# The leaky step of finished rows: relu on ScalarE and a linear part from TensorE in place of one VectorE operation

## The reference, cut to what matters

```
t = proj[src, etype];  h = proj[dst, etype]          # x @ relation_weight
att = sum(t * tanh(h + edge_attr))                   # softmax over the edges of one dst
h_nb = segment_sum(x[src] * softmax(att))
g = leaky_relu((x + h_nb) @ W1.T, 0.01) + leaky_relu((x * h_nb) @ W2.T, 0.01)
out = layernorm(x + g)
```

## Time and profile before

| what | value |
|---|---|
| median of 3 runs | 764.09 us (762.74 to 765.07) |
| span of the profiled execution | 764.9 us |
| DVE busy | 634.8 us (83%) |
| POOL busy | 581.8 us (76%) |
| PE busy | 556.2 us (73%) |
| ACT busy | 499.1 us (65%) |
| mean granted TensorE clock | 0.917 |

### The profile page before, as it was taken

How to read it: one execution, slowest core, us unless ns; L and a number is a source line. 1 busy time by engine, 2 the same in 40 slices (tenths; PEclk the granted TensorE clock), 3 DMA queues, 4 the chain that set the end, 5 groups by cost and what they waited for, 6 DMA issues and landing times. The chain is left out here.

```text
span 764.9 us, 14665 instructions
## 1 busy us (share of the span) xinstructions
PE 556.2 (73%) x3780; PEld 293.9 (38%) x3780; DVE 634.8 (83%) x1115; ACT 499.1 (65%) x1474; POOL 581.8 (76%) x590
## 2 busy tenths in 40 slices
PE   1887888888789788888889887788888788632000
PEld 0652454445345345345345343333333333321000
DVE  1689999999999999999999999999999899742010
ACT  0366677679778779779778777765656446755040
POOL 6777777777777777777777777777777777777776
PEclk9999999999999999999999999999999999755555
DMA  5463435434434434434444332422112221000000
GB/s 134 105 191 81 124 89 144 124 87 145 124 95 137 125 106 126 133 106 117 138 107 115 104 104 73 108 73 75 48 46 74 75 83 44 28 26 17 19 18 16
DMA packets 49457, 70.41 MB, mean 92 GB/s; under 512 B 17450, under 2 KB 20966, under 8 KB 49374
## 3 DMA queue, kind: packets, MB, share of 16 engines
q1 hardware_dynamic: 30750, 52.33, 21.2%
q0 software_dynamic: 18624, 17.16, 10.9%
HBM read 45.61 MB, written 25.78 MB: 93 GB/s over the span
## 5 line engine op out<-in xcount | busy, mean ns | idle before, releaser
L441 POOL DMA_INDIRECT xsd<-in_x,ends_i x384 | 378.2, 985 | 118.0 <-issue 108.6
L543 PE MATMUL t_ps<-xm,w_rel 64*64 64x512 f32 (+1 forms) x1000 | 270.3, 622 | 39.7 <-DVE xm L912 39.2
L912 DVE SCALAR_TENSOR_TENSOR xm<-typ,xT_ps 128x1024 f32<-128x1024 f32 (+1 forms) x250 | 292.4, 1187 | 2.6 <-issue 2.6
L545 PE MATMUL h_ps<-xm,w_rel 64*64 64x512 f32 (+1 forms) x1000 | 270.2, 622 | 0.0
L465 POOL DMA_INDIRECT out<-out_r,row_i x196 | 200.6, 1023 | 59.7 <-issue 55.5
L560 PE MATMUL y_ps<-bd_cat,dT 128*128 128x256 f32 x392 | 97.9, 394 | 17.6 <-DVE zd L974 14.8
L691 ACT ACTIVATE o_t<-zd,rstd 128x64 f32<-128x64 f32 x392 | 98.8, 337 | 14.9 <-DVE rstd L996 14.9
L543 PEld LDWEIGHTS t_ps<-xm,w_rel 64*64 64x64 f32 x1000 | 52.7, 135 | 142.7 <-DVE xm L912 117.4
L578 PE MATMUL s_ps<-bd_both,uwT 128*128 128x128 f32 x392 | 73.4, 313 | 36.6 <-issue 35.9
L578 PEld LDWEIGHTS s_ps<-bd_both,uwT 128*128 128x128 f32 x392 | 54.9, 203 | 115.1 <-issue 95.3
L560 PEld LDWEIGHTS y_ps<-bd_cat,dT 128*128 128x128 f32 x392 | 72.5, 195 | 30.9 <-issue 12.8
(11 more groups left out here) (143 smaller groups left out, 742.1 us busy)
## 6 DMA issues: line engine op xcount, KB each, us to landing
xsd<-in_x SPq DMA_DIRECT2D x1024, 0.2 KB
x_in<-in_x SPq DMA_DIRECT2D x48, 256.0 KB
typ<-typ_d SPq DMA_DIRECT2D x24, 512.0 KB
out<-o_t SPq DMA_DIRECT2D x48, 256.0 KB
xsd<-in_x,ends_i POOLq DMA_INDIRECT x384
hist<-es SPq DMA_DIRECT2D x24, 256.0 KB, 2.0
ea<-in_edge_attr SPq DMA_DIRECT2D x24, 224.0 KB
out<-out_r,row_i POOLq DMA_INDIRECT x196, 2.1
```

The lines of the kernel that those rows point to most:

```text
L441: pool.indirect_dma_start(xsd[:, s % RX, j, side, :], None, x[:, :], bass.IndirectOffsetOnAxis(ap=ends_i[:, side, c:c + 1], axis=0),).then ...
L543: pe.matmul(t_ps[h * D:(h + 1) * D, 0:n], w_rel[0:D, r, :], xm[0:D, b, h * n:(h + 1) * n], start=(r == 0), stop=(r == R - 1), skip_group_c ...
L545: mm = pe.matmul(h_ps[(1 - h) * D:(2 - h) * D, 0:n], w_rel[D:P, r, :], xm[D:P, b, (1 - h) * n:(2 - h) * n], start=False, stop=(r == R - 1) ...
L912: v.scalar_tensor_tensor(xm[:, (s * R + r) % RM, 0:n], typ[:, s % RT, 0:n], float(r), xT_ps[:, 0:n], ALU.is_equal, ALU.mult).then_inc(mask ...
```

## The change

The quarters no longer go through `l12`. With y1 and y2 the two products, leaky(y1) + leaky(y2) is 0.99 relu(y1) + 0.99 relu(y2) + 0.01 (y1 + y2). PE multiplies with `bd_sum`, three blocks of 64 columns: 0.99 y1, 0.99 y2 and 0.01 (y1 + y2). ACT takes relu of the first block into `r1`. DVE adds max(second block, 0) to it, straight from PSUM (`relu_add`), and then the third block (`linear_add`). `zf` becomes double buffered. The quarter's place in PSUM is free only after linear_add, so PE waits on `zlin_done` where it waited on `pf_done`. PE's order changes: pair_y 1 goes behind dense_y(D1), pair_y 2 behind quad 8, and pair_y 3 behind dense_y(D2), with the marks for POOL to match. ACT's order stays as it is.

```diff
-        YQ = 256
+        YQ, YW = 128, 3 * D
+        def y_part(k):
+            return s_ps[:, YQ:YQ + 2 * YW].rearrange("p (j k f) -> p j k f", j=2, k=3)[:, :, k, :]
 (pair_y, PE)
-                wait(pe, pf_done, Q_BEFORE[f] + q)
+                wait(pe, zlin_done, Q_BEFORE[f] + q)
-                    mm = pe.matmul(s_ps[:, YQ + j * P:YQ + (j + 1) * P], uwT[:, q // 2, k * P:(k + 1) * P], bd_both[:, :],
-                                   start=True, stop=True)
+                    mm = pe.matmul(s_ps[:, YQ + j * YW:YQ + (j + 1) * YW], uwT[:, q // 2, k * P:(k + 1) * P],
+                                   bd_sum.rearrange("p k f -> p (k f)"), start=True, stop=True)
 (PE's order in a step)
+                if D1 is not None:
+                    dense_y(D1)
                 if quarters > 1:
                     pair_y(f, 1)
-                if D1 is not None:
-                    dense_y(D1)
                 if main:
                     quad(s, 7)
-                if quarters > 2:
-                    pair_y(f, 2)
                 if D2 is not None:
                     dense_turn(D2)
                 if main:
                     quad(s, 8)
+                if quarters > 2:
+                    pair_y(f, 2)
...
-                if quarters > 3:
-                    pair_y(f, 3)
                 if D2 is not None:
                     dense_y(D2)
+                if quarters > 3:
+                    pair_y(f, 3)
 (pair_out, ACT)
-                wait(act, z1_done, f)
-                act.copy(l12[:, 2 * q:2 * q + 2, :, :],
-                         s_ps[:, YQ:YQ + 2 * P].rearrange("p (j k f) -> p j k f", j=2, k=2)).then_inc(pf_done, 1)
+                wait(act, r12_done, Q_BEFORE[f])
+                act.activation(r1[:, 2 * q:2 * q + 2, :], y_part(0), ACT.Relu).then_inc(pf_done, 1)
 (DVE)
-            def leaky(f):
-                ...
-                v.scalar_tensor_tensor(l, l, SLOPE, l, ALU.mult, ALU.max).then_inc(l_done, 1)
-            def final_add(f):
-                ...
-                v.tensor_tensor(zf[:, 0:n, :], l12[:, 0:n, 0, :], l12[:, 0:n, 1, :], ALU.add).then_inc(z1_done, 1)
+            def relu_add(f, q):
+                v.wait_ge(pf_done, Q_BEFORE[f] + q + 1)
+                v.scalar_tensor_tensor(zf[:, f % 2, 2 * q:2 * q + 2, :], y_part(1), 0.0, r1[:, 2 * q:2 * q + 2, :],
+                                       ALU.max, ALU.add).then_inc(r12_done, 1)
+            def linear_add(f, q):
+                v.wait_ge(r12_done, Q_BEFORE[f] + q + 1)
+                z = zf[:, f % 2, 2 * q:2 * q + 2, :]
+                v.tensor_tensor(z, z, y_part(2), ALU.add).then_inc(zlin_done, 1)
```

More of the change, by code:

```diff
@@ L116, in gnn_resnorm @@
         bd_both = sb("bd_both", [P, P])
+        bd_sum = sb("bd_sum", [P, 3, D])
         ends_i = sb("ends_i", [P, 2, T], I32)
@@ L161, in gnn_resnorm @@
         uwT = sb("uwT", [P, 2, 512])
-        l12 = sb("l12", [P, COLS, 2, D])
-        zf = sb("zf", [P, COLS, D])
+        r1 = sb("r1", [P, COLS, D])
+        zf = sb("zf", [P, 2, COLS, D])
         zs = sb("zs", [P, COLS])
@@ L206, in gnn_resnorm @@
         h_done, uw_done, y12_done, pf_done = sem("h_done"), sem("uw_done"), sem("y12_done"), sem("pf_done")
-        l_done, z1_done, z2_done, fsum_done, fsub_done = sem("l_done"), sem("z1_done"), sem("z2_done"), sem("fsum_done"), sem("fsub_done")
+        r12_done, zlin_done, z2_done, fsum_done, fsub_done = sem("r12_done"), sem("zlin_done"), sem("z2_done"), sem("fsum_done"), sem("fsub_done")
         fsq_done, red2_done, fmul_done, xfix_done = sem("fsq_done"), sem("red2_done"), sem("fmul_done"), sem("xfix_done")
         fx_pe, fx_v, fx_act, end_in, fix_out = sem("fx_pe"), sem("fx_v"), sem("fx_act"), sem("end_in"), sem("fix_out")
+        def y_part(k):
+            return s_ps[:, YQ:YQ + 2 * YW].rearrange("p (j k f) -> p j k f", j=2, k=3)[:, :, k, :]
         def turn(n, ring):
@@ L270, in pe_marks @@
                 quads(6, 7)
+                multiplied(1)
                 paired(1)
-                multiplied(1)
                 quads(7, 8)
-                paired(2)
                 turned(2)
                 quads(8, 9)
+                paired(2)
+                multiplied(2)
                 paired(3)
-                multiplied(2)
                 quads(9, 10)
@@ L500, in _ @@
                       start=True, stop=True).then_inc(last_done, 1)
-            pe.wait_ge(setup_w, 7)
+            pe.wait_ge(setup_w, 12)
             def turn_in(s):
@@ L518, in scores @@
                 if e >= 2:
-                    pe.wait_ge(pf_done, Q_BEFORE[e - 1])
+                    pe.wait_ge(zlin_done, Q_BEFORE[e - 1])
                 half = cols(e) // 2
@@ L834, in _ @@
             v.memset(bd_both[:, :], 0.0).then_inc(setup_w, 1)
+            v.memset(bd_sum[:, :, :], 0.0).then_inc(setup_w, 1)
             v.memset(ones2[:, :], 0.0).then_inc(setup_m, 1)
@@ L852, in _ @@
             v.wait_ge(resT, 1)
-            v.wait_ge(setup_w, 2)
+            v.wait_ge(setup_w, 3)
             for h in range(2):
@@ L857, in _ @@
                 v.tensor_copy(bd_both[q, q], s_ps[q, D:2 * D]).then_inc(setup_w, 1)
-            v.wait_ge(setup_w, 6)
+                v.tensor_scalar(bd_sum[q, h, :], s_ps[q, D:2 * D], 1.0 - SLOPE, None, ALU.mult).then_inc(setup_w, 1)
+                v.tensor_scalar(bd_sum[q, 2, :], s_ps[q, D:2 * D], SLOPE, None, ALU.mult).then_inc(setup_w, 1)
+            v.wait_ge(setup_w, 11)
             v.scalar_tensor_tensor(bd_cat[:, 1, :], bd_cat[:, 0, :], SLOPE, ident[:, :], ALU.mult, ALU.add).then_inc(setup_w, 1)
@@ L1005, in pair @@
                 v.tensor_tensor(uw[:, 0:n, 1, :], h_t[:, 0:n, :], xd, ALU.mult).then_inc(uw_done, 1)
-            def leaky(f):
-                n = cols(f)
-                v.wait_ge(pf_done, Q_BEFORE[f + 1])
-                l = l12[:, 0:n, :, :].rearrange("p j k f -> p (j k f)")
-                v.scalar_tensor_tensor(l, l, SLOPE, l, ALU.mult, ALU.max).then_inc(l_done, 1)
-            def final_add(f):
-                n = cols(f)
-                v.wait_ge(l_done, f + 1)
-                v.tensor_tensor(zf[:, 0:n, :], l12[:, 0:n, 0, :], l12[:, 0:n, 1, :], ALU.add).then_inc(z1_done, 1)
+            def relu_add(f, q):
[6 more added lines that the diff above has]
+                v.tensor_tensor(z, z, y_part(2), ALU.add).then_inc(zlin_done, 1)
             def final_add_x(f):
                 n = cols(f)
-                v.wait_ge(z1_done, f + 1)
-                v.tensor_tensor(zf[:, 0:n, :], zf[:, 0:n, :], xsd[:, f % RX, 0:n, 1, :], ALU.add).then_inc(z2_done, 1)
+                v.wait_ge(zlin_done, Q_BEFORE[f + 1])
+                v.tensor_tensor(zf[:, f % 2, 0:n, :], zf[:, f % 2, 0:n, :], xsd[:, f % RX, 0:n, 1, :], ALU.add).then_inc(z2_done, 1)
             def final_sum(f):
@@ L1025, in final_sum @@
                 v.wait_ge(z2_done, f + 1)
-                v.tensor_reduce(zs[:, 0:n], zf[:, 0:n, :], AX.X, ALU.add).then_inc(fsum_done, 1)
+                v.tensor_reduce(zs[:, 0:n], zf[:, f % 2, 0:n, :], AX.X, ALU.add).then_inc(fsum_done, 1)
             def final_centre(f):
@@ L1032, in final_centre @@
                 v.scalar_tensor_tensor(zcf[:, f % 2, 0:n, :], zs[:, 0:n].unsqueeze(2).to_broadcast([P, n, D]), -1.0 / D,
-                                       zf[:, 0:n, :], ALU.mult, ALU.add).then_inc(fsub_done, 1)
+                                       zf[:, f % 2, 0:n, :], ALU.mult, ALU.add).then_inc(fsub_done, 1)
             def final_squares(f):
@@ L1046, in _ @@
                 on, ending, late = 0 <= e < NS, 0 <= f < NS, 0 <= l < NS
+                quarters = 2 * groups(f) if ending else 0
                 if DP is not None:
@@ L1090, in _ @@
                     mask(s, 7)
+                if quarters > 0:
+                    relu_add(f, 0)
                 if on:
                     sum_one(e, 4)
+                if quarters > 0:
+                    linear_add(f, 0)
+                if on:
                     sum_one(e, 5)
@@ L1103, in _ @@
                     sum_one(e, 6)
+                if quarters > 1:
+                    relu_add(f, 1)
+                if on:
                     sum_one(e, 7)
+                if quarters > 1:
+                    linear_add(f, 1)
                 if main:
@@ L1108, in _ @@
                     dense_add(D1)
+                if quarters > 2:
+                    relu_add(f, 2)
                 if D1 is not None:
                     dense_total(D1)
+                if quarters > 2:
+                    linear_add(f, 2)
                 if D1 is not None:
@@ L1124, in _ @@
                     inverse(e)
-                if ending:
-                    leaky(f)
-                    final_add(f)
                 if main:
                     product(s)
+                if quarters > 3:
+                    relu_add(f, 3)
+                if D0 is not None:
+                    dense_sum(D0)
+                if quarters > 3:
+                    linear_add(f, 3)
```

(2 more changed lines are left out.)

## The result

The changed kernel takes 791.6 us (median of 4 runs, 790.58 to 794.78) against 764.58 us of the kernel before in the same comparison: ratio 1.0358, 95% interval 1.0331 to 1.0385, slower. That is 27 us; the forecast was 24, and the range held it.

What follows compares the result with a forecast made beforehand. POOL's issue rate was taken as the bound. Steps 2 to 14 add 34.5 us and step 15 0.6, 35.1 in all; minus 11.4 of slack, POOL is 23.7 us late: 788 us predicted, range 771 to 803.

Steps and rivals of the forecast that it cites:

- POOL bounds the kernel, by its issue rate: POOL issues back to back from first gather to end; other engines' gains can't shorten the kernel.
- DVE's own work: Per step, 1.81 us removed and eight 128-element operations of 0.21 us added, partly filling holes: about 0.7 us shorter.
- rival 2: DVE alone decides, 0.5 us a step slower by full durations, under the slack: 764 us; 0.13 together with rival 1.
- The walk: Second half of step 11 through PE, ACT and DVE queues: stalls at relu_add 2 and product, step 2.8 us longer.
- the tail: DVE behind product to the next step's first mask: 3.70 us as before plus 0.55 for the last quarter.
- The 13 steps: Steps 2 to 14, each taken as 31.0 us: 13 x 31.0 - 368.5 = 34.5 us added.
- Step 15 and later: Step 15 grows by 0.6 us, later steps by about 1 us each, covered by the scatters' slack.
- The slack of 11.4 us: At gather 380, waiting for quad 4 of step 16: compute may be 11.4 us later before POOL waits.
- the threshold of 0.83 us a step: Growth of each of steps 2 to 14 below which POOL never waits and the end stays.
- 1: Rival: no change, 764 us, as the chain is shorter and step growth stays under 0.83 us; 0.13 together with rival 2.
- 3: Rival: DVE bounds the kernel, its 0.7 us a step is won: 17 us, 747; 0.04 with anything else faster.
- Rival 4: Stalls add up: relu_add 0 and 1 both miss by 0.5 us, step 3.8 us longer, some 802 us; chance 0.10.

Runs made afterwards that it cites:

- v_reordered: Changed kernel with PE, ACT and DVE work put in another order, same data path: 758.4 us, ratio 0.9928 against the kernel before.
- a_neither_wait: Changed kernel with rows scattered into a second DRAM tensor, without the wait for dense stores, and LEAD 1250 instead of 250: 784.5 us, ratio 1.0249.
- a_pace_loose: Changed kernel with LEAD 1250 instead of 250, so that gathers hardly wait for PE: 792.3 us, ratio 1.0377.
- v_pe_act_only: Changed kernel with pair_y 3 behind quad 9, dense_copy(D2) ahead of relu 2 and relu 3 behind tanh, DVE's order kept: 774.0 us, ratio 1.0138.
- b_pace_loose: Kernel before the change, with LEAD 1250 instead of 250: 763.4 us, ratio 1.0000.

## Why the prediction was right, point by point

- **POOL bounds the kernel, by its issue rate.** Right, and shown by v_reordered: a step that is 0.6 us shorter on average (27.74 against 28.34) leaves POOL's idle time unchanged.
- **DVE's own work.** Right. relu_add 0 takes 0.21 us from its start to the next one's (369.58 to 369.79 in DVE's rows above), as forecast, though it lasts 0.28; the sum of 64 elements behind it takes 0.19, not 0.15. Without its waits (0.81 and 2.32) the step would take 27.6 us, 0.6 less than before (0.7 forecast). The full durations of rival 2 would have made it more than before.
- **The walk.** Right at every station, with each wait a little over-estimated: dense_copy(D2) 1.73 us late (1.7 forecast), relu_add 2 0.81 us idle (1.0), product 2.32 us idle (2.6) and 2.04 us late (2.27), the tail 4.23 us (4.25), the full step 30.76 us (31.0).
- **The 13 steps.** 28.5 us were added and not 34.5. Half of the difference is the usual step, 30.76 and not 31.0 us (13 times 0.24). The other half is that too many steps were taken as equal: steps 2 to 4 take 29.8 us, and in steps 3 and 4 relu_add 2 doesn't wait. By the code, final_out on ACT begins only with step 5; that this is the reason was not tested.
- **Step 15 and later.** Step 15 grew by 0.8 (0.6 forecast), step 16 by 3.3 and the steps from 17 on mostly by 2.4 us (1 forecast), with DVE idle 1.7 us before product. That was covered in the kernel after and is not in a_neither_wait, where unfinished rows cost 18.9 us. Of DVE's 26.5 us of cover at the end 5 were to be left, and none is, but POOL's last scatter still follows the one before it by 0.30 us.
- **The slack of 11.4 us.** This step failed. It is the slack of the pace, and behind it stood the store of the last dense tile with 1.2 us. By a_pace_loose the store alone sets the first scatter, whatever the pace does, and by v_pe_act_only the threshold of 0.83 us a step, worked out from the 11.4, does not exist. The prediction expected no wait in the scatters; the first one waits 9.3 us. Two errors met: 28.5 instead of 34.5 us of added steps, and 1.2 instead of 11.4 us of slack. With them the first scatter is 28.8 us late instead of 23.7. By the pace alone POOL is 19.8 us late (gather 380).
- **What POOL's instructions cost.** Taken as fixed. The scatters' mean fell from 1023 to 998 ns (196 x 25 ns = 4.9 us), which brought 28.8 back to 23.8 us. That the profiled span of 788.6 us is the predicted one to the digit is an accident of three errors. The medians differ by 27.0 us and not by 24. The rest is which executions were profiled. In every run with both numbers the time is 1.7 to 2.2 us above the span, so the execution profiled before took some 767 us (an estimate from its span of 764.9). That is longer than any recorded time of that kernel and some 2.2 us above its median, while the one profiled after was the fastest of four (790.58), 1.0 below its median. These two differences are the missing 3.2. Some of the 12.6 us by which POOL's instructions are shorter is therefore the choice of execution, and that the forecast lies 4 us from the median is luck in part.
- **Rivals.** 1 and 3 fell with the 30.76 us and POOL's idle time, 2 with DVE's own work. Rival 4 fell: relu_add 0 and 1 find their inputs in the walked step.

## What to carry to other kernels

When work is cut into pieces that go from engine to engine and back through one buffer, walk one period with the queues in order, and look at what stands behind each new wait: here a copy that another engine needed, behind a relu that was not ready, cost 1.1 of 2.6 us. Where one engine issues without a gap, list every wait in its program, not only the one that looks like a throttle; the nearest one counts, and relaxing the others only moves the same wait. A change that frees the busiest engine and makes the kernel slower may need only its order mended; but where another engine sets the time, what it frees is no gain by itself. And before two traces are subtracted, hold each one's time against its kernel's median: here that was 3 of 27 us.

## What had not been expected of the hardware

POOL's indirect DMA instructions are mostly 0.94 us (gathers) and 0.97 us (scatters), but some are much longer, up to 2.07 us before and 2.76 us in v_reordered. Their means differ with the same work: 985 and 1023 ns before, 971 and 999 in v_reordered, though POOL waits for nothing in either. That is 10 us, but not all of it belongs to the kernels. In b_pace_loose, where the median is that of the kernel before, the means are 980 and 1009 ns, 4.8 us less in all than in the trace of before. The medians leave 5.0 us between the kernel before and v_reordered. No run was made on the cause, and it stays open.

TensorE's granted clock can fall, step after step, in a kernel whose engines are busy nearly all the time: in the kernel after its mean is 0.94 over step 11 and over the three steps behind it. At the start of step 11 matmul records take 1.11 us where the same work took 0.64 before, when the mean over the step was 1.00. Just ahead of that stretch PE had idled 0.28 us for linear_add 3 and 0.89 us for dense_add(D2); before, it had idled 0.77 us for dense_add(D2) alone, and the clock stayed up. Here the fall cost nothing, since DVE was the later one there.
